# A stream of attention steps: where a group's end puts one mix, one output projection and the weight splits

## The reference

```python
def reference(...):
    def _L0_attn_b_ref(x, Wq, Wk, Wv, Wo, q_norm_w, k_norm_w):
        H, HKV, HD = (32, 8, 128)
        q = (x @ Wq.T).reshape(b, s, H, HD).transpose(0, 2, 1, 3)
        k = (x @ Wk.T).reshape(b, s, HKV, HD).transpose(0, 2, 1, 3)
        v = (x @ Wv.T).reshape(b, s, HKV, HD).transpose(0, 2, 1, 3)
        q = _rmsnorm(q, q_norm_w)
        k = _rmsnorm(k, k_norm_w)
        qg = q.reshape(b, HKV, G, s, HD)
        scores = jnp.einsum('bkgqd,bksd->bkgqs', qg, k) / math.sqrt(HD)
        bias = jnp.where(rel > 0, NEG_INF, slopes[:, :, None, None] * rel)
        attn = jax.nn.softmax(scores + bias[None], axis=-1)
        out = jnp.einsum('bkgqs,bksd->bkgqd', attn, v)
        out = out.reshape(b, H, s, HD).transpose(0, 2, 1, 3).reshape(b, s, H * HD)
        return out @ Wo.T
    x = L0_attn_a_x                                   # (1, 1024, 512), float32
    x = x + _L0_attn_a_ref(_layernorm(x, axis=-1), ...)
    x = x + _L0_ffn_ref(_layernorm(x, axis=-1), ...)
    x = x + _L0_attn_b_ref(_layernorm(x, axis=-1), ...)
    x = x + _L0_ffn_ref(_layernorm(x, axis=-1), ...)
    return x
```

## Time and profile before

| | us |
|---|---|
| median of 3 runs | 1602.74 |
| lowest, highest | 1601.39, 1602.80 |
| the profiled execution | 1604.81 |
| its span, first to last instruction | 1603.0 |
| mean granted clock of TensorE, of 1 | 0.984 |

### The profile page before, as it was taken

The page is one execution under the profiler, slowest core; times in us unless marked ns, Lnnn a source line. Parts: engine busy times, 40 slices in busy tenths (PEclk is TensorE's granted clock), DMA queues, the critical chain, the costliest instruction groups (busy, mean ns, idle before and its releaser), DMA issues.

```text
span 1603.0 us, 25452 instructions
## 1 busy us (share of the span) xinstructions
PE 1507.2 (94%) x8968; PEld 1174.6 (73%) x8968; DVE 1111.8 (69%) x2866; ACT 796.5 (50%) x2087; POOL 440.3 (27%) x435
## 2 busy tenths in 40 slices
PE   3998999998897899999999999999999999999997
PEld 2863444443686788888888888888888888888776
DVE  5658777771575577687678677678767767767873
ACT  3522555557333355555555555555554555555441
POOL 4102000010452341341332234144134143224332
PEclk9997999999999899999999999999999999999999
DMA  4363344301100100100100010010010010000000
GB/s 150 96 140 56 41 61 59 43 2 54 54 21 1 40 27 1 40 21 8 40 14 14 1 40 27 1 40 27 1 40 27 1 40 14 14 19 22 7 21 27
DMA packets 40206, 54.27 MB, mean 34 GB/s; under 512 B 5776, under 2 KB 21392, under 8 KB 40080
## 3 DMA queue, kind: packets, MB, share of 16 engines
q1 hardware_dynamic: 40080, 52.65, 13.8%
HBM read 44.04 MB, written 8.39 MB: 33 GB/s over the span
## 4 chain that ended last, share of the span: by engine, by line
PE 65%; DVE 3%; issue 2%; POOL 2%; ACT 2%; POOLq 0%; ACTq 0%; DVEq 0%
PE ps L50 18%; PE ps L52 18%; PE ps L51 18%; PE ps L1528 7%; PE ps L1503 2%; DVE ab_qt_l L1777 1%; POOL ab_o_l L1424 1%; PE ps L241 1%; PE ps L1505 0%; ACT ab_o_raw L1695 0%; POOL wo L1392 0%; ACT ab_kt_h L1674 0%; POOL ab_o_h L1422 0%; DVE ab_pt_l L1785 0%; ACT ab_squares L1665 0%
## 5 line engine op out<-in xcount | busy, mean ns | idle before, releaser
L1653 ACT ACTIVATE prob<-prob,ab_neg_max 128x128 f32<-128x128 f32 (+7 forms) x256 | 200.7, 784 | 241.7 <-DVE ab_neg_max L1768 240.6
L1785 DVE TENSOR_TENSOR ab_pt_l<-ps,ab_pt_h 128x512 fp32r<-128x512 f32 x288 | 198.0, 688 | 67.3 <-ACT ab_pt_h L1681 65.0
L1681 ACT CAST ab_pt_h<-ps 128x512 fp32r<-128x512 f32 x288 | 171.7, 596 | 127.2 <-PE ps L1528 126.6
L1768 DVE CUSTOM_DVE_ANT_0 prob<-ps,rel 128x512 f32<-128x512 f32 (+3 forms) x256 | 146.1, 571 | 102.6 <-PE ps L52 101.8
L50 PE MATMUL ps<-ab_w_h,ab_xt_h 128*128 128x512 f32 (+1 forms) x512 | 185.6, 362 | 5.0 <-DVE ab_v_l L1805 5.0
L1041 DVE TENSOR_REDUCE ra_part_max<-ps 128x1 f32<-128x512 f32 (+3 forms) x318 | 156.4, 552 | 48.3 <-PE ps L943 29.2
L1528 PE MATMUL ps<-ident,prob 128*128 128x128 f32 x1152 | 173.4, 273 | 4.6 <-DVE ab_qt_l L1777 3.3
L52 PE MATMUL ps<-ab_w_h,ab_xt_l 128*128 128x512 f32 (+1 forms) x512 | 174.4, 341 | 0.0
L51 PE MATMUL ps<-ab_w_l,ab_xt_h 128*128 128x512 f32 (+1 forms) x512 | 173.7, 339 | 0.0
L1793 DVE TENSOR_SCALAR prob<-prob,ab_recip 128x128 f32<-128x128 f32 (+7 forms) x256 | 164.1, 641 | 9.1
L1413 POOL TENSOR_TENSOR ab_rms<-ab_ms_eps,neg_half 128x5 f32<-128x5 f32 x64 | 76.3, 1192 | 318.0 <-DVE ab_ms_eps L1810 317.2
(11 more groups left out here) (232 smaller groups left out, 3487.9 us busy)
## 6 DMA issues: line engine op xcount, KB each, us to landing
f_raw<-in_wqkv SPq DMA_DIRECT2D x32, 384.0 KB, 3.7
f_raw<-in_wbo SPq DMA_DIRECT2D x32, 256.0 KB, 2.6
ra_first_rows<-parts SPq DMA_DIRECT2D x36, 128.0 KB, 6.7
parts<-pa_stage SPq DMA_DIRECT2D x12, 256.0 KB, 3.1
parts<-f_raw SPq DMA_DIRECT2D x12, 256.0 KB, 3.3
ra_q_st<-parts SPq DMA_DIRECT2D x24, 128.0 KB, 6.5
ra_k_st<-parts SPq DMA_DIRECT2D x24, 128.0 KB, 6.8
f_raw<-in_wf SPq DMA_DIRECT2D x8, 324.0 KB, 3.3
```

The source lines that it names most:

```text
L1653: act.activation(prob[:, t % 2, h, 0:w], prob[:, t % 2, h, 0:w], ACT.Exp, bias=neg_max[:, t % 2, h, pieces_per_head(t % NT) - 1:pieces_per ...
L1681: act.copy(pt_h[:, n % PT, :], ring_bank("p", u, j)).then_inc(pt_high, 1)
L1768: dve.tensor_tensor_reduce(out=prob[:, t % 2, h, k0:k1], in0=ps[:, n % 2, a:b], in1=const["rel"][:, SLIDE - i * P + k0:SLIDE - i * P + k1] ...
L1785: dve.tensor_tensor(pt_l[:, n % PT, :], ring_bank("p", u, j), pt_h[:, n % PT, :].bitcast(F32), ALU.subtract).then_inc(emptied, 1)
```

## The change

Five edits, all in `stream_block` and the functions of (t, s) that it calls:
- `mixed_in`: the only mix of a group's first tile (u = 8g) moves from slot 4 to slot 6 of step 8g+1. ScalarE's copy `ab_o_raw` of that tile follows from slot 5 to slot 7.
- `output_in`, new: the output projection of a group's last tile (u = 8g-1), and VectorE's addition, move from slot 7 of step 8g+1 to slot 0 of step 8g+2, for the first seven groups. The jobs keep their order in the ring of banks.
- ScalarE's casts of `wo` move from slot 7 of step 8g+1 (two) and slots 0 and 1 of step 8g+2 (one each) to slot 1 (three) and slot 3 (one) of step 8g+2. GpSimd's subtractions keep their places.
- `qk_high` counts the casts of q and k apart, so that it rises by two a step.
- `qk_low_of` waits for the first count before `ab_qt_l` and for the second before `ab_kt_l`.

```diff
--- before.py
+++ after.py
@@ -1117,8 +1117,18 @@
 
 def mixed_in(t, s):
 
+
     u, j = (t - 1, s - 4) if s >= 4 else (t - 2, s + B_SLOTS - 4)
-    return (u, j) if 0 <= u < B_STEPS and j <= u % NT else None
+    if u % NT == 0:
+        j -= 2
+    return (u, j) if 0 <= u < B_STEPS and 0 <= j <= u % NT else None
+
+
+def output_in(t, s):
+
+    late = t - 3 if s == 0 else t - 2
+    u = late if s in (0, 7) and 0 <= late < B_STEPS else None
+    return u if u is not None and (s == 0) == (u < B_STEPS - NT and u % NT == NT - 1) else None
 
 
 def taken_in(t, s):
@@ -1149,8 +1159,8 @@
                 add(t, "k", t + 1)
             if turned_in(t, s):
                 add(t, "p", *turned_in(t, s))
-            if s == 7 and 0 <= t - 2 < B_STEPS:
-                add(t, "o", t - 2)
+            if output_in(t, s) is not None:
+                add(t, "o", output_in(t, s))
             half, q = half_of(t, s)
             b, = second_tiles(half, 2)
             if b is not None and q == weighted_quarter(b):
@@ -1585,8 +1595,8 @@
                         project(t + 2, s)
                     if mixed_in(t, s):
                         mix(*mixed_in(t, s))
-                    if s == 7 and 0 <= t - 2 < B_STEPS:
-                        project_out(t - 2)
+                    if output_in(t, s) is not None:
+                        project_out(output_in(t, s))
                     second(*half_of(t, s))
 
             def middle(m):
@@ -1670,7 +1680,7 @@
 
             def qk_high_of(t):
                 act.wait_ge(qk_turned, t + 1)
-                act.copy(qt_h[:, t % 2, :, :], ring_bank("q", t).rearrange("p (h t) -> p h t", h=GB))
+                act.copy(qt_h[:, t % 2, :, :], ring_bank("q", t).rearrange("p (h t) -> p h t", h=GB)).then_inc(qk_high, 1)
                 act.copy(kt_h[:, key_columns(t)], ring_bank("k", t)[:, 0:P]).then_inc(qk_high, 1)
 
             def pt_high_of(u, j):
@@ -1702,13 +1712,13 @@
                     if s == 4 and DEFERRED <= t + 2 < B_STEPS:
                         squares_of(t + 2)
                     g, i = divmod(t, NT)
-                    if i == 1 and s == 7 and 0 <= g < KVB:
+                    if i == 2 and s == 1 and 0 <= g < KVB:
                         if g:
                             act.wait_ge(out_done, NT * g)
-                        split_high_of(2 * KC * g + KC)
-                        split_high_of(2 * KC * g + KC + 1)
-                    if i == 2 and s < 2 and 0 <= g < KVB:
-                        split_high_of(2 * KC * g + KC + 2 + s)
+                        for k in range(KC - 1):
+                            split_high_of(2 * KC * g + KC + k)
+                    if i == 2 and s == 3 and 0 <= g < KVB:
+                        split_high_of(2 * KC * g + 2 * KC - 1)
                     if t == SECOND - 1 and s < KC:
 
                         act.wait_ge(projected, KC * (SECOND + 1))
@@ -1773,9 +1783,10 @@
                                          accum_out=neg_max[:, t % 2, h, c:c + 1]).then_inc(shifted, 1)
 
             def qk_low_of(t):
-                dve.wait_ge(qk_high, t + 1)
+                dve.wait_ge(qk_high, 2 * t + 1)
                 dve.tensor_tensor(qt_l[:, t % 2, :, :], ring_bank("q", t).rearrange("p (h t) -> p h t", h=GB),
                                   qt_h[:, t % 2, :, :].bitcast(F32), ALU.subtract).then_inc(emptied, 1)
+                dve.wait_ge(qk_high, 2 * t + 2)
                 dve.tensor_tensor(kt_l[:, key_columns(t)], ring_bank("k", t)[:, 0:P],
                                   kt_h[:, key_columns(t)].bitcast(F32), ALU.subtract).then_inc(emptied, 1)
 
@@ -1864,8 +1875,8 @@
                     if s == 6 and DEFERRED <= t + 2 < B_STEPS:
                         scale_qk(t + 2)
                     second(*half_of(t, s))
-                    if s == 7 and 0 <= t - 2 < B_STEPS:
-                        u = t - 2
+                    if output_in(t, s) is not None:
+                        u = output_in(t, s)
                         dve.wait_ge(out_done, u + 1)
                         if u >= NT:
                             dve.wait_ge(emptied, job_of["o", u - NT][0] + 1)
```

## The result

| | before | changed |
|---|---|---|
| median, us | 1602.77 | 1639.86 |
| lowest, highest | 1601.39, 1602.94 | 1637.93, 1640.31 |
| ratio, with 95% interval | | 1.0231 (1.0213 to 1.0249) |
| span of the profiled execution | 1603.0 | 1638.1 |

The changed kernel is 2.3% slower: 37.1 us, where 36.0 were forecast, and 1639.86 us where 1638.7 were. The page's first lines give the same picture: the span is 35 us longer (the profiled execution of the kernel before, at 1604.81 us, stands 2.0 above that kernel's median, the changed kernel's on its median), and TensorE's busy share has fallen, against the earlier trace rows.

The account below looks back on a forecast made before the run. TensorE is busy 94% of the span, so only what stops it costs time. Seven groups x (1.91 + 1.70 + 1.79 - 0.32 = 5.08) = 35.6, + 0.4 for group 0 = 36.0: 1638.7 us, range 1616 to 1655.

Parts of the forecast that it names:

- late mix, stop for `ab_o_raw`: Group's end: with the mix behind the last score, its wait shrinks from 0.49 to 0.14 us, gaining 0.35 us a group.
- stop for `ab_v_l`: Step 8g+2's first projection, its covering matmuls moved away, waits for VectorE to empty the projection banks: TensorE stands 3.15 us.
- first stop at full clock, a group: Moving the mix and output projection costs 1.91 us a group up to the moved projection's end, gains of both included.
- low clock, seven groups: After each 3.15 us stop TensorE's granted clock falls, costing 1.7 us a group, with ends 0 and 3.4.
- second stop, by the starts: Next output projection waits 1.70 us for `ab_o_l` behind the late fourth cast; 1.79 us a group with its first matmul.
- q and k, a group: Counting q's and k's casts apart starts `ab_qt_l` 0.16 us earlier at about two waits: gain 0.32 us a group.
- group 0: Only the weight split's 1.79 us, less 0.32 and two casts of 0.55 no longer ahead of ScalarE's squares: +0.4 us.
- My bracket for the length at which it falls: TensorE's granted clock held after 1.66 us of idle and fell after 2.58, so the edge lies between.
- The clock held: Rival: no low clock after the seven 3.15 us stops, so without 7 x 1.7 us: 1627 us; chance 15%.
- it stays low for longer: Rival: low clock at both stops of a group, or for longer, 8 x 1.7 us more: 1652 us; chance 15%.
- The weights didn't stay hidden: Rival that they do: ScalarE or GpSimd reach the fourth part sooner, without 8 x 1.79 us: 1624 us; chance 12%.
- The two old waits did vanish: Rival: the waits at the group's end just vanish, with `ab_scaled` and weights in time, 11.7 us less: 1591 us; chance 5%.

Follow-up runs that it names:

- e6: The changed kernel with 11 needless 512-column matmuls in front of the projection quarter that waits for `ab_scaled`, seven times: 1627.76 us, ratio 1.0153.
- e4: The kernel before with one edit, the casts of q and k counted apart so `ab_qt_l` waits for q's alone: 1600.70 us, ratio 0.9983.
- e2: The kernel before with only the output projection of tile 8g-1 moved to slot 0 of step 8g+2, behind the first projection quarter: 1634.36 us, ratio 1.0193.
- e9: The changed kernel with the moved output projection ahead of the first projection quarter in slot 0, and the casts of `wo` at their old places: 1596.90 us.
- e7: The changed kernel with GpSimd's `ab_rms` ahead of `ab_o_h` and `ab_o_l` in step 8g+1, g from 1 to 7: 1628.97 us, ratio 1.0160.
- e3: The changed kernel with the fourth cast of `wo` right behind the third, in slot 1 of step 8g+2 instead of slot 3: 1626.06 us, ratio 1.0141.
- e10: The kernel of e8 with all four casts of `wo` in slot 1 of step 8g+2: 1592.77 us, ratio 0.9941 to the kernel before.
- e5: The kernel before with one edit, the mix of tile 8g in slot 6 instead of 4 of step 8g+1: 1602.67 us, ratio 0.9997.
- e8: The changed kernel with output projection and `wo` casts at their old places, and eight matmuls on `ab_o_h` ahead of the wait for `ab_o_l`: 1595.37 us.

## Why the prediction was right, step by step

| step | forecast, us | measured, us | from |
|---|---|---|---|
| late mix, stop for `ab_o_raw` | 0.49 to 0.14 | 0.14 | start 654.37 |
| stop for `ab_v_l` | 3.15 | 3.15, seven times | start 658.85, e6 |
| first stop at full clock, a group | 1.91 | 1.93 | steps 41 and 42, e6 |
| low clock, seven groups | 11.9 | 12.3 | lags at L1513; 12.1 by e6 |
| second stop, by the starts | 1.70 | 1.86 | start 675.02 |
| q and k, a group | 0.32 | 0.35 | e4 |
| group 0 | +0.4 | -0.96 | step 9 |
| sum | 36.0 | 36.3 | lag at L1513 in step 62 |
| time | 36.0 | 37.1; 35.1 in the span | medians; pages |

The sum of the steps is right to 0.3 us, but two errors of more than 1 us cancel in it: the seven groups cost 5.31 us each where I had 5.08 (1.6 us more in all), and group 0 gave 1 us where I had a loss (1.4 less). Behind step 62 the changed kernel stays 36.3 us behind up to VectorE's last addition (1634.94 against 1598.66); only what comes behind it, the last transfer out, takes 1.2 us less, and that makes the 35.1 of the span. The 37.1 of the medians have in them the 2.0 us by which the profiled execution of before lay above its median. That 36.0 and 37.1 are so close is in part luck.

*Cover.* The decisive step was to ask what the moved 2.81 us of matmuls had been hiding. Before, `ab_v_l` was 0.7 us early; e2 shows that the move alone costs 31 us, with the clock and the 0.6 us for `ab_qt_l`, and e9 that a move into the same slot costs nothing when the cover stays.

*Clock.* The mean came out right, but partly by luck: I took one stretch of low clock for each of seven stops. There was none once, a short one three times (1.5 us) and a long one three times (2.5 to 2.7 us, up to 6.1 us from the projection's start on, not 4). e6 shows the cause; nothing here says why stops of the same length end differently, and in e7 they even alternate. That stays open. My bracket for the length at which it falls, 1.66 to 2.58 us, also passed over a row of the same trace, of group 0:

```profile
518.23 1.05 PE L241 MATMUL ps<-ident,ab_xn 128*128 128x128 f32 x4 [1.87 <-DVE ab_xn L233]
```

The four transposes take 1.05 us where they take 0.66 after the same stop of 1.87 us in e2 and e4, and the granted clock of 518 to 520 is 0.59. The lower clock had come after 1.87 us of idle, and it lasted through the stop of 522.64 until 528.8. So a stop of 1.7 us, which I took to be free of it, was closer to the edge than I said; after the seven in the steady part the clock did hold.

*Second stop.* It was there, where and why I said: e3 removes most of it. It was 0.16 us longer, for the most part since the cast of `ab_o_h` behind the fourth part took 0.74 us (672.88) where I had 0.61. With its slower first matmul it costs 1.95 us, against 1.79. The 0.32 for q and k fits: 1.93 for the first stop, 1.76 for the mean of the clock and 1.95, less 0.33, are the 5.31 us a group that were measured. The weight loads' waits for `ab_qt_l` don't halve, as I had said, but are gone from the list; by the starts some 0.1 us of each is left (668.98 to 669.18, where 0.12 would be no wait).

*Group 0.* Here the step failed in its sign. I counted two casts less ahead of ScalarE's squares (1.1 us) and left out the clock. The second stop is there as forecast (535.04, 1.70 us of idle) and costs 1.95 us. On the other side stand the projection behind `ab_v_l` and what follows it, before and after:

```profile
522.64 0.80 PE L50 MATMUL ps<-ab_w_h,ab_xt_h 128*128 128x512 f32 x1 [2.40 <-DVE ab_v_l L1805]
...
527.61 1.05 PE L1503 MATMUL ps<-ident,ab_nat 128*128 128x128 f32 x4
```

```profile
521.26 0.65 PE L50 MATMUL ps<-ab_w_h,ab_xt_h 128*128 128x512 f32 x1 [2.72 <-DVE ab_v_l L1816]
...
525.54 0.60 PE L1513 MATMUL ps<-ident,ab_nat 128*128 128x128 f32 x4
```

The squares start 1.37 us earlier (517.18 against 518.55) and the projection 1.38, where I had 1.1. The same work up to the transposes of q then takes 4.28 us instead of 4.97, and from there to the next wait's end (530.46, 527.74) 2.20 instead of 2.85: of this 0.69 + 0.42 = 1.1 us is clock, since both executions run this stretch at the lower level but the one of before does so until 528.8, the changed one until 524.9. With 1.38 and 1.1 gained, 0.4 for q and k in both steps and 1.95 lost, the 0.96 us come out. How much of the 1.1 is the change and how much this one execution of before, whose clock fell early at 518.23, no run isolates. e3 and e10, which also draw the fourth cast forward, are 5.1 to 5.3 us ahead at step 9 (0.6 to 0.8 of it was there at the first transposes): they have no second stop there, and the clock held after the stop of 2.58 us at 538.65, after which it fell in all the others.

*The rivals.* The clock held in one group of seven, so that rival was wrong as a whole and right in a seventh; that it stays low for longer came true in three of seven, but never after the second stop. The weights didn't stay hidden. The range's lower end, 1616, also lay above the 1614 that it was drawn from. The two old waits did vanish, and it earned nothing by itself, as e5 shows for one of them: the engine arrives earlier at the next wait.

## What to carry to other kernels

A wait on the busiest engine can be followed by work that covers another engine's chain, as here; before that work is moved, look at what stands next in its place and how early its operand is. If a late operand has parts, use those that are ready (e8) rather than move the whole. And a stop of TensorE of 2.4 us or more cost another 1.4 to 2.8 us in clock in most places here, while the waits of 0.3 to 1.7 us in the steady part cost none: an order that gathers the waiting in one long stop pays for it twice.

## What the runs showed of the hardware

After a stop of 2.4 or 3.0 us of idle TensorE's granted clock fell in most cases, but not in all: 6 of 7 with 3.0 (the changed kernel), 7 of 7 with 3.0 (e2 and e3), 4 of 7 with 2.4 (e7), never in the steady part behind the 1.7 us stops. In group 0 it fell once after 1.87 us (before, 518.23) and held twice after the same stop (e2, e4). The lower level cost 1.4 to 1.6 us for a short stretch and 2.5 to 2.8 for a long one, by the lags at L1513. Needless matmuls in the stop kept the clock up at no cost in time (e6). The Trainium skill (TensorE: Matmul & The Clock Gate, Why this matters for your kernels) asks to avoid idle gaps between bursts of matmuls, but only above a length that the stops of e7 don't reach; after four of those the clock fell all the same, and the measurement decides.
